# SyncE's issue order in a gated cross-attention kernel: one context block and the result store change places

## The reference

```python
q, k, v = layernorm(x) @ Wq + bq, ctx @ Wk + bk, ctx @ Wv + bv
energy = where(mask == 0, lowest, einsum('nqhd,nkhd->nhqk', q, k))
a = softmax(energy / sqrt(16)) @ v
x = x + tanh(g_xattn) * (a @ Wo + bo)
x = x + tanh(g_ffn) * tanh(layernorm(x) @ W1 @ W2 @ W3 + b_ffn)
```

## Time and profile before

| | |
|---|---|
| time, median of 3 runs | 1083.36 us (1081.43 to 1085.96) |
| profiled execution | 1079.94 us |
| its span in the trace | 1078.1 us |
| TensorE busy | 1023.4 us, 95% |
| VectorE busy | 948.6 us, 88% |
| ScalarE, GpSimd busy | 77%, 75% |
| DMA issued by SP | 155.72 MB |

### The profile page before, as it was taken

One profiled execution on the slowest core, in us unless ns is written; L12 is line 12 of the kernel. 1 busy time (PEld: TensorE's weight loads), 2 busy tenths in 40 slices (PEclk: granted clock), 3 DMA queues, 4 the chain that ended last, 5 costly groups with the idle time before them and its releaser, 6 DMA issues.

```text
span 1078.1 us, 45335 instructions
## 1 busy us (share of the span) xinstructions
PE 1023.4 (95%) x18487; PEld 892.2 (83%) x18487; DVE 948.6 (88%) x1331; ACT 828.6 (77%) x1275; POOL 806.0 (75%) x1184
## 2 busy tenths in 40 slices
PE   5988999999999999999999999999999999999965
PEld 5777888888888888888888888888888888888855
DVE  5778999998899999989999998899998999999866
ACT  4566888888788888878888788788887887878742
POOL 5245878878788887878888877788787887888753
PEclk9999999999999999999999999999999999999998
DMA  5133555555555555555555556555555555555431
GB/s 154 45 104 106 165 147 161 162 155 152 155 153 164 145 171 155 164 149 149 165 154 162 157 145 173 143 161 159 152 164 150 150 163 149 167 152 154 124 124 69
DMA packets 260400, 158.87 MB, mean 147 GB/s; under 512 B 174945, under 2 KB 227170, under 8 KB 260194
## 3 DMA queue, kind: packets, MB, share of 16 engines
q1 hardware_dynamic: 260050, 155.72, 51.4%
q10 hardware_dynamic: 144, 0.26, 0.1%
HBM read 85.92 MB, written 68.94 MB: 144 GB/s over the span
## 4 chain that ended last, share of the span: by engine, by line
PE 55%; DMA 13%; SPq 13%; issue 7%; POOL 6%; DVE 5%; ACT 1%; POOLq 0%; DVEq 0%; ACTq 0%
PE ps_m L507 11%; PE ps_m L500 11%; PE ps_s L636 9%; PE ps_s L615 8%; PE ps_x L647 7%; PE ps_m L574 5%; DMA scratch_y<-yn 5%; SPq L215 3%; DMA scratch_m<-max_T 3%; PE ps_s L621 3%; SPq L303 2%; SPq L292 2%; DMA q_aug<-scratch_m 2%; PE ps_m L494 2%; DMA den_wide<-scratch_r 2%
## 5 line engine op out<-in xcount | busy, mean ns | idle before, releaser
L1021 DVE TENSOR_TENSOR probs<-ps_s,far_T 128x2048 f32<-128x2048 f32 x128 | 293.3, 2291 | 60.0 <-PE ps_s L636 59.8
L1010 DVE TENSOR_REDUCE neg_max<-ps_s 128x16 f32<-128x2048 f32 x128 | 292.5, 2285 | 26.7 <-PE ps_s L621 26.2
L810 ACT ACTIVATE probs<-probs 128x2048 f32<-128x2048 f32 x128 | 245.0, 1914 | 6.2 <-DVE probs L1021 5.9
L785 ACT ACTIVATE q_aug<-ps_m,q_bias,q_scale 128x256 f32<-128x256 f32 x256 | 123.5, 563 | 58.0 <-PE ps_m L500 48.9
L615 PE MATMUL ps_s<-k_aug,q_aug 32*128 32x128 f32 x4096 | 150.6, 283 | 14.2 <-DVE probs L1021 8.1
L636 PE MATMUL ps_s<-q_aug,k_aug 32*128 32x128 f32 x4096 | 152.1, 283 | 8.5 <-DMA q_aug<-scratch_m 5.8
L615 PEld LDWEIGHTS ps_s<-k_aug,q_aug 32*128 32x128 f32 x4096 | 127.9, 186 | 34.9 <-issue 24.3
L636 PEld LDWEIGHTS ps_s<-q_aug,k_aug 32*128 32x128 f32 x4096 | 127.7, 186 | 27.3 <-DMA q_aug<-scratch_m 9.4
L647 PE MATMUL ps_x<-probs,v_ones 128*32 128x128 f32 x4096 | 139.2, 277 | 3.2 <-issue 2.4
L785 ACT ACTIVATE k_aug<-ps_m,k_bias,parity 128x256 f32<-128x256 f32 x256 | 123.5, 563 | 18.8 <-PE ps_m L500 18.8
L647 PEld LDWEIGHTS ps_x<-probs,v_ones 128*32 128x32 f32 x4096 | 104.7, 110 | 32.7 <-issue 32.6
(11 more groups left out here) (123 smaller groups left out, 1725.9 us busy)
## 6 DMA issues: line engine op xcount, KB each, us to landing
scratch_a<-a_den SPq DMA_DIRECT2D x64, 512.0 KB, 3.7
x_in<-in_x SPq DMA_DIRECT2D x64, 256.0 KB, 4.4
a_rows<-scratch_a SPq DMA_DIRECT2D x64, 256.0 KB
den_wide<-scratch_r SPq DMA_DIRECT2D x64, 256.0 KB
out<-y SPq DMA_DIRECT2D x64, 256.0 KB, 4.7
ctx_in<-in_ctx SPq DMA_DIRECT2D x252, 64.0 KB, 2.7
scratch_y<-yn SPq DMA_DIRECT2D x59, 256.0 KB, 4.3
y_blocks<-scratch_y SPq DMA_DIRECT2D x236, 64.0 KB, 2.4
```

The costliest lines, as they stand in the source:

```text
L785: last = nc.scalar.activation(dst[:, :, 2 * m + a, :], src[:, m * TOK:(m + 1) * TOK].rearrange("p (n q) -> p n q", q=P), ACT.Identity, bia ...
L810: nc.scalar.activation(tile, tile, ACT.Exp).then_inc(probs_ready, 1)
L1010: nc.vector.tensor_reduce(neg_max[:, 0:H].rearrange("p (j c) -> p j c", j=G), ps_s[:], AX.X, ALU.max, negate=True).then_inc(max_ready, 1)
L1021: nc.vector.tensor_tensor(probs[i % 2][:].rearrange("p j s q -> p (j s) q"), ps_s[:].rearrange("p j s q -> p (j s) q"), far_T[:].unsqueeze ...
```

## The change

In turn t, the first of the four blocks of `load_ctx(t+3)` is issued between `read_den(t-2)` and `read_max(2t)`; the other three stay behind `load_x(t+4)`. The store moves from the start of a turn to its second half, behind `read_a` and ahead of `write_y`, and stores pair t-6 there, where the start of the next turn stored the same pair before. No other engine's instructions change.

```diff
-            def load_ctx(p):
+            def load_ctx_blocks(p, blocks):
                 wait(sp, ctx_turned, p - 1)
-                if p == 0:
-                    sp.dma_start(ctx_in[0][:], ctx_v[:, 0]).then_inc(ctx_landed[0], 16)
-                    return
-                for a in range(G):
+                for a in blocks:
                     rows = slice(a * 32, (a + 1) * 32)
                     sp.dma_start(ctx_in[p % 2][rows].rearrange("c n (b e) -> c (n b) e", e=64),
...
+            def load_ctx(p):
+                if p == 0:
+                    sp.dma_start(ctx_in[0][:], ctx_v[:, 0]).then_inc(ctx_landed[0], 16)
+                else:
+                    load_ctx_blocks(p, range(G))
...
             for t in range(NP):
-                if is_pair(t - 7):
-                    store(t - 7)
                 if is_pair(t - 5):
                     read_y(t - 5)
                 write_max(2 * t)
                 if is_pair(t - 2):
                     read_den(t - 2)
+                if is_pair(t + 3):
+                    load_ctx_blocks(t + 3, (0,))
                 read_max(2 * t)
                 if is_pair(t - 2):
                     write_a(t - 2)
                 if is_pair(t + 4):
                     load_x(t + 4)
                 if is_pair(t + 3):
-                    load_ctx(t + 3)
+                    load_ctx_blocks(t + 3, (1, 2, 3))
                 write_max(2 * t + 1)
                 if is_pair(t - 2):
                     write_reciprocals(t - 2)
                     read_a(t - 2)
+                if is_pair(t - 6):
+                    store(t - 6)
                 if is_pair(t - 4) and t - 4 <= END:
                     write_y(t - 4)
                 read_max(2 * t + 1)
                 if is_pair(t - 2):
                     read_wide(t - 2)
             y3, y2, y1, last = NP - 4, NP - 3, NP - 2, NP - 1
-            store(NP - 7)
             read_den(y1)
```

## The result

The changed kernel takes 1106.66 us (median of 4 runs, 1103.39 to 1111.52); the kernel before, on the same chip, 1082.39 us. The ratio is 1.0219, 95% interval 1.0189 to 1.0249: slower by 2.2%, 24 us, where 1104.5 us was forecast. The profiled execution is the slowest of the four, 1111.52 us, and the one profiled before, 1079.94 us, is 2.5 us under its median, so the two traces overstate the loss by some 7 us: their spans differ by 31.6 us, the medians by 24.3.

What follows compares the result with a forecast made beforehand. SP's loop was taken to bound the turn as much as TensorE; store +0.70 and context block -0.32 give +0.38 us over 55 turns, 21 us, so the 1083.36 us median becomes 1104.5, range 1074 to 1122.

Steps and rivals of the forecast that it cites:

- What bounds: SP's loop, 15.89 us, level with TensorE's 15.67: added time lengthens the turn, savings give at most 0.19 us a turn.
- The context block: One block's issue (0.49 us) moves into the wait before the even read_max, which holds 0.32: -0.32 us a turn.
- The store: Ahead of write_y: issue 0.24 us net plus data up to 0.93; between 0 and 1.17, taken as +0.70 us.
- The choice near the upper bound: Store's term taken as 0.70 of at most 1.17 us, because write_y already queues behind read_a.
- The sum: SP's loop changes by +0.70 - 0.32 = +0.38 us a turn; over 55 turns, 21 us slower.
- 8 engines full and 8 empty: In write_y's flight, the DMA engines' 0.49 use looks like 8 full and 8 empty, not 16 at half load.
- A: Faster: idle DMA engines take the store, its term under 0.32 us; 10.5 us less, 1073 us; chance 0.20.
- B: No change: the store's term is near the context block's 0.32 us; 1083 us, from 1078 to 1088; chance 0.12.
- C: Slower: store's data wait in full, context pocket gives little; 1.07 us a turn at worst, 0.8 likelier, 1127 us; chance 0.13.

Runs made afterwards that it cites:

- the runs without the data: Stores in the loop write only 16 of 128 partitions (32 KB): in the changed kernel 0.9949; in the kernel with only the store moved 0.9968.

## Why the prediction was right

**What bounds.** Right, and the basis of all the rest: SP's loop from write_y to write_y was level with TensorE's order, so that a loss counts in full and a gain is capped. The asymmetry shows in the same edit, the context block, which is worth 0.015 on top of the store and 0.005 on top of the kernel before. The cap is tighter than the 0.19 us forecast: of TensorE's 10.1 idle us in 900, 7 to 8 remain in both runs of the context block alone (892.05 and 893.04 busy), of which the maxima's arrival ended 1.8 us in one run and none in the other. I had put all 10.1 down to SP, and in the kernel before the maxima's arrival ended only 4.1 of them.

**The context block.** Forecast -0.32 us a turn where SP's loop bounds; between the store alone and the change it measured 16.39 - 16.69 = -0.30. The pocket was filled as said: the wait for the maxima's landing fell from 17.9 to 0.7 us. That the size came out so well is partly luck. In the means of turns 8 to 59, the stretch from write_a to the odd write_max shrank by 4.03 - 3.26 = 0.77 us, not by 0.49, mostly because a block's issue takes 0.60 us in the mean (four took 2.39 and three 1.83) and not the 0.45 of the round that I had read. The even read_max came 2.42 - 2.05 = 0.37 us later and not 0.17, because with the store in place its pocket held next to nothing (4.2 us in 900). The rest of the loop grew by 0.1 us.

**The store.** Forecast +0.70 us between 0 and 1.17; measured 16.69 - 15.86 = +0.83 by the traces, with whatever the clock's falls cost in it, and 0.70 by the ratio. The size was right and the parts were not; that their errors cancel is luck. The issue does delay write_y's start, by 1.24 - 0.95 = 0.29 us against 0.24 forecast, but by the runs without the data this does not reach its landing and costs nothing (0.9968). The data delay the landing by 1.02 us, about their full 0.93 and not the 0.46 that the 0.70 left for them. Of this some 0.2 us a turn came back elsewhere: the even read_max waited less for its write to land (17.9 us in 900 before, 4.2 with the store alone), a pocket that the forecast spent on the context block alone. The choice near the upper bound rested on the queue behind read_a; the runs with smaller stores (0.9949, 1.0019, 1.0219 for 32, 128 and 256 KB) and with other places (0.9972, 1.0036, 1.0219) bear that out.

**The sum.** +0.38 forecast; the medians give 24.3 / 55 = +0.44, and the profiled executions, 16.39 - 15.86 = +0.53.

**The mechanism.** "8 engines full and 8 empty" is argued and not shown: the pattern meant to put the store on 8 engines costs 0.9% more than the other at equal bytes, as it should, but it also writes to other places, and 8 engines loaded as by the full store did not give the full store's loss. The rule of the Trainium skill (DMA: Bandwidth & Descriptors, on why a DMA increments its semaphore by 16) agrees in direction with that pair of runs; no row here shows which engines a transfer took.

**What the changed profile was to show.** TensorE's idle time 34 us (forecast 30), 25.4 us of it ahead of the odd scores_T and ended by `q_aug<-scratch_m`; the wait for yn gone; write_y issued 1.21 us behind read_a (forecast 1.2) and its landing 6.13 us behind it in the mean (forecast 5.7 to 6.2); the even read_max no longer waits; the turn 16.39 us (forecast 16.2). All of these came.

**The rivals.** A, idle engines take the store, fell: the store's term is 0.70 to 0.83, far from the 0.32 at which it decides. B fell with it. C, the whole price, fell as a sum, 1.07 at worst against 0.44 to 0.53 measured; but its reason, that the store's data wait in full, is what the landings show.

## What to carry to other kernels

Where one engine's queue issues every transfer, write down its loop from one round trip to the next and mark which idle times are pockets (work there is free) and which are slack: waits for a landing that the loop needs are pockets, and data put ahead of that landing lengthen it even if the issue is free. Put bulk stores behind the round trip's write and behind small reads that another engine waits for; here, each time with the context block moved as well, the kernel with the same 256 KB ahead of the write was 2.2% slower than before, just behind it 0.4% slower, and behind both 0.3% faster. Before moving a load later, look up when its first user runs, since the price of missing that is not the transfer's but a turn's order.

Of the orders run here that write the whole output, the context block alone is the fastest: 0.9952 and 0.9948 of the kernel before in two runs.

## What the runs showed of the hardware that was not expected

Two stores of 128 KB in rows of 2 KB, one written as 64 rows in one piece and one as 8 groups of 8 in places apart, differ by 0.9% of the kernel's time (1.0019 and 1.0112), and in issue by 0.54 against 0.65 us. The length of rows between 1 and 2 KB made no difference that the intervals can tell (1.0219 and 1.0264, 1.0189 to 1.0249 and 1.0227 to 1.0302).

Behind a 256 KB read, a 256 KB write that was issued 0.35 us later landed at the same time (5.11 and 5.12 us behind the read's start in one trace each; two traces of one kernel differ by up to 0.16), while 256 KB more of data between the two made it land 1.02 us later.

TensorE's granted clock fell to 0.50, its level of 1.2 GHz, for short stretches in the middle of the kernel with the store alone, five times between 120 and 1020 us, never there in the kernel before. Ahead of the fall shown TensorE was busy for 1.66 of 3.40 us, and ahead of the other four for 0.95 to 1.65 of 3.40. Its waits can so cost more than their own length; that they caused the falls is not shown.
